# Transformer layer on one core: scores, states, own values and carried values of TensorE's batches put into one stretch of small tiles

## The reference, cut to what matters

```python
def _L0_attn_ref(hidden_states, rel_pos, Wq, Wk, Wv, Wo):     # 8 heads of 16
    q, k, v = (split_heads(hidden_states @ W) for W in (Wq, Wk, Wv))
    # per head, chunks of C = 64 tokens, gamma = 1 - 2**(-5-head):
    attn    = (qc @ kc.T) * D              # D = gamma**(i-j) where i >= j
    o_intra = attn @ vc
    o_inter = (qc * decay_q) @ S
    S_new   = decay_s * S + (kc * decay_k).T @ vc
    return o @ Wo

def _L0_ffn_ref(x, ...):
    h = bitlinear(x, w_fc) + gate * (x @ v.T @ fast_b.T @ u.T)
    r = maximum(h, 0)
    return bitlinear(r * r, w_proj)

xn = layernorm(x)                          # x: 8 x 512 x 128, float32
return x + attn(xn) + ffn(xn)
```

## Time and profile before

| what | value |
|---|---|
| median of 3 runs | 129.23 us (128.18 to 129.38) |
| the profiled execution's own time | 129.01 us |
| its span, from the first to the last instruction | 127.0 us |
| TensorE busy | 117.0 us (92%) |
| VectorE busy | 99.2 us (78%) |
| ScalarE busy | 78.7 us (62%) |
| GpSimd busy | 64.0 us (50%) |
| granted TensorE clock, mean | 0.997 |

### The profile page before, as it was taken

The page is one execution under the profiler, slowest core; times in us unless marked ns, Lnnn a source line. Parts: engine busy times, 40 slices in busy tenths (PEclk is TensorE's granted clock), DMA queues, the critical chain, the costliest instruction groups (busy, mean ns, idle before and its releaser), DMA issues.

```text
span 127.0 us, 6564 instructions
## 1 busy us (share of the span) xinstructions
PE 117.0 (92%) x2860; PEld 92.8 (73%) x2860; DVE 99.2 (78%) x261; ACT 78.7 (62%) x158; POOL 64.0 (50%) x60
## 2 busy tenths in 40 slices
PE   4979999988999999499999999999999999499991
PEld 4425869856688778377788778878897889377890
DVE  0788795489799969858699979896999799729832
ACT  3265669967871897227972897188738774382910
POOL 7099803984439161923439252916193529544400
PEclk9999999999999999999999999999999999999998
DMA  3849920000023000400023001300020002000202
GB/s 105 296 149 320 389 92 34 0 3 5 8 90 81 5 0 23 145 7 0 0 92 74 0 0 53 112 0 0 0 83 0 0 0 83 0 5 0 88 5 83
DMA packets 3357, 7.71 MB, mean 61 GB/s; under 512 B 384, under 2 KB 896, under 8 KB 3216
## 3 DMA queue, kind: packets, MB, share of 16 engines
q1 hardware_dynamic: 2880, 7.01, 16.3%
q10 hardware_dynamic: 464, 0.50, 1.2%
HBM read 5.42 MB, written 2.10 MB: 59 GB/s over the span
## 4 chain that ended last, share of the span: by engine, by line
PE 80%; DVE 10%; issue 4%; ACT 2%; POOL 1%; DVEq 0%; POOLq 0%
PE ps_work L659 10%; PE ps_score L735 8%; PE ps_work L663 7%; PE ps_work L660 7%; PE ps_score L705 6%; PE ps_score L747 5%; PE ps_score L781 5%; PE ps_y L761 4%; PE ps_y L762 4%; PE ps_score L720 3%; DVE sums_of L532 3%; PE ps_turn L668 3%; PE ps_y L765 2%; DVE xn L491 2%; PE ps_turn L692 1%
## 5 line engine op out<-in xcount | busy, mean ns | idle before, releaser
L300 POOL TENSOR_TENSOR sq_lo<-square,sq_hi 128x512 fp32r<-128x512 f32 x31 | 39.8, 1295 | 36.2 <-ACT sq_hi L356 36.2
L347 ACT ACTIVATE square<-ps_work 128x512 f32<-128x512 f32 x32 | 19.1, 596 | 23.1 <-PE ps_work L663 22.6
L516 DVE TENSOR_TENSOR scores<-ps_score,cst 128x512 f32<-128x512 f32 x32 | 20.3, 682 | 1.6 <-PE ps_score L705 1.6
L305 POOL TENSOR_TENSOR q_pair<-q_dec,cst 128x1024 f32<-128x1024 f32 x7 | 13.3, 1894 | 15.9 <-DVE q_dec L501 15.9
L356 ACT ACTIVATE sq_hi<-square 128x512 fp32r<-128x512 f32 x32 | 20.1, 627 | 0.1
L352 ACT ACTIVATE square<-square 128x512 f32<-128x512 f32 x32 | 18.9, 630 | 0.1
L491 DVE TENSOR_SCALAR xn<-x_in,mean_var,rstd 128x128 f32<-128x128 f32 x32 | 14.9, 528 | 0.3
L659 PE MATMUL ps_work<-xn_hi,w_hi 128*128 128x512 f32 x32 | 14.3, 447 | 0.4 <-issue 0.4
L735 PE MATMUL ps_score<-scores,v_pad 64*32 64x64 f32 x1024 | 12.5, 225 | 1.6 <-issue 1.6
L663 PE MATMUL ps_work<-xn_lo,w_hi 128*128 128x512 f32 x32 | 12.6, 394 | 0.0
L660 PE MATMUL ps_work<-xn_hi,w_lo 128*128 128x512 f32 x32 | 12.6, 393 | 0.0
(11 more groups left out here) (123 smaller groups left out, 238.6 us busy)
## 6 DMA issues: line engine op xcount, KB each, us to landing
x_in<-x_tok SPq DMA_DIRECT2D x8, 256.0 KB, 3.4
resid<-x_feat SPq DMA_DIRECT2D x1, 2048.0 KB, 7.7
out_feat<-resid SPq DMA_DIRECT2D x7, 256.0 KB
po_in<-ffn_weights SPq DMA_DIRECT2D x1, 320.0 KB, 3.2
fc_in<-ffn_weights SPq DMA_DIRECT2D x1, 256.0 KB, 3.7
q_table<-q_decay SPq DMA_DIRECT2D x1, 256.0 KB, 3.5
wqvk<-qvk_weights ACTq DMA_DIRECT2D x1, 192.0 KB, 3.9
cst<-const ACTq DMA_DIRECT2D x1, 129.0 KB, 3.9
```

What stands on the lines that cost most here:

```text
L300: nc.gpsimd.tensor_tensor(sq_lo[p][:, f, :], square[p][:, f, :], sq_hi[p][:, f, :].bitcast(F32), ALU.subtract).then_inc(lo_ready, 1)
L347: nc.scalar.activation(square[b.parity][:, f, :], ps_work[f % 2][:], ACT.Relu).then_inc(relu_ready, 1)
L516: nc.vector.tensor_tensor(scores[:, g].rearrange("p t s i -> p (t s) i"), ps_score[:, g].rearrange("p (a i) -> p a i", i=BLK), causal.unsq ...
```

## The change: what it does

- TensorE runs hidden 0 to 3 of b in a row. Then the four sets of small products stand in one stretch: score of b, gather states of b, own values of b - 1, carry of b - 1. Then turn of b + 1, second product and output product of b - 1, and q, k, v of b + 1.
- Own values go one batch later, so `scores` gets a second buffer. `own_values(first)` leaves the prologue; the code for the last batch holds own values twice (of batch 6 and of batch 7).
- PSUM: the attention output and the states move from ps_score into two banks of their own, ps_out. ps_turn and ps_y are now the third and fourth bank of ps_score, and the two v sides use its first and second. So turn, second product, q/k/v and score wait for the masks, for `take_v` and for `finish` that read those banks.
- VectorE's order in a body: statistics of b + 1, `take_v` of side 1 of b, variance, roots, normalise, four masks, `low_o`, `low_xn`, states of b and their sums, `decay_q`, `finish`, `take_v` of side 0. ScalarE takes all four relus before the squares. GpSimd's list is as it was.
- In the prologue VectorE copies w2, wo_full and wo_hi in place of ScalarE, and sums the states of batch 0 before it takes v of batch 1.

```diff
-        scores = sb("scores", [P, NG, NT, PAIR, BLK])
+        scores = [sb(f"scores{p}", [P, NG, NT, PAIR, BLK]) for p in range(2)]
...
         ps_score = pb("ps_score", [P, NG, SEQ])
+        ps_out = pb("ps_out", [P, ROWS, SEQ])
         ps_work = [pb(f"ps_work{p}", [P, SEQ]) for p in range(2)]
-        ps_turn = pb("ps_turn", [P, SEQ])
-        ps_y = pb("ps_y", [P, SEQ])
+        ps_turn, ps_y = ps_score[:, 2], ps_score[:, 3]
+
+        first_turn, ps_w1 = ps_out[:, 0], ps_out[:, 1]
...
-            return (ps_turn if side == 0 else other)[:].rearrange("p (w t d) -> p w t d", w=2, t=2)
+            if b is first:
+                bank = first_turn if side == 0 else ps_work[0][:]
+            else:
+                bank = ps_score[:, side]
+            return bank.rearrange("p (w t d) -> p w t d", w=2, t=2)
...
-        o_bank = ps_score[:, 0:ROWS, 0:NT * BLK].rearrange("p r (t i) -> p t r i", i=BLK)
+        o_bank = ps_out[:, :, 0:NT * BLK].rearrange("p r (t i) -> p t r i", i=BLK)
+        state_bank = ps_out[:, :, NT * BLK:NT * (BLK + GW)]
...
             take_relu(first, 3)
             round_xn(first.step(1))
             high_square(first, 0)
-            act.wait_ge(proj_turned, 1)
-            nc.scalar.activation(w2[:], ps_y[:].rearrange("p (t d) -> p t d", d=D), ACT.Copy).then_inc(w2_copied, 1)
             high_square(first, 1)
             take_square(first, 2)
-            act.wait_ge(wo_turned, 1)
-            nc.scalar.activation(wo_full[:], ps_y[:, 0:D], ACT.Copy)
-            nc.scalar.activation(wo_hi[:], ps_y[:, 0:D], ACT.Copy).then_inc(wo_rounded, 1)
-            take_square(first, 3)
-            high_square(first, 2)
             copy_k(first.step(1))
             copy_k_tok(first.step(1), 0)
+            take_square(first, 3)
             copy_k_tok(first.step(1), 1)
+            high_square(first, 2)
             high_square(first, 3)
 
             def body(b):
                 take_relu(b, 0)
                 take_relu(b, 1)
                 root(b.step(1))
-                take_square(b, 0)
-                take_square(b, 1)
-                high_square(b, 0)
+                take_relu(b, 2)
+                take_relu(b, 3)
+                for f in range(3):
+                    take_square(b, f)
+                    high_square(b, f)
                 high_o(b.step(-1))
-                take_relu(b, 2)
-                high_square(b, 1)
                 round_xn(b.step(1))
-                take_relu(b, 3)
-                take_square(b, 2)
                 take_square(b, 3)
-                high_square(b, 2)
+                high_square(b, 3)
                 copy_k(b.step(1))
                 copy_k_tok(b.step(1), 0)
-                high_square(b, 3)
                 copy_k_tok(b.step(1), 1)
...
-            take_relu(last, 0)
-            take_square(last, 0)
-            high_o(last.step(-1))
-            high_square(last, 0)
-            for f in range(1, NF):
+            for f in range(NF):
                 take_relu(last, f)
+            for f in range(3):
                 take_square(last, f)
                 high_square(last, f)
+            high_o(last.step(-1))
+            take_square(last, 3)
+            high_square(last, 3)
...
             nc.vector.tensor_scalar(wo_scaled[:], wo_in, inv_scale2[:], None, ALU.mult).then_inc(wo_ready, 1)
+            dve.wait_ge(proj_turned, 1)
+            nc.vector.tensor_copy(w2[:], ps_score[:, 1].rearrange("p (t d) -> p t d", d=D)).then_inc(w2_copied, 1)
             low_xn(after)
+            dve.wait_ge(wo_turned, 1)
+            nc.vector.tensor_copy(wo_full[:], ps_y[:, 0:D])
+            nc.vector.tensor_copy(wo_hi[:], ps_y[:, 0:D]).then_inc(wo_rounded, 1)
             decay_q(after)
             dve.wait_ge(wo_rounded, 1)
             nc.vector.tensor_tensor(wo_lo[:], ps_y[:, 0:D], wo_hi[:].bitcast(F32), ALU.subtract).then_inc(y_free, 1)
+            take_states(first)
+            for k in range(3):
+                add_states(first, k)
             take_v(after, 0)
-            take_v(after, 1)
             dve.wait_ge(resid_loaded, 16)
 
             def body(b):
                 before, after = b.step(-1), b.step(1)
                 statistics(after)
                 statistics_done(after)
-                take_states(before)
+                take_v(b, 1)
                 variance(after)
-                for k in range(3):
-                    add_states(before, k)
                 for step in range(4):
                     inverse_root(after, step)
                 normalise(after)
+                for g in MASK_ORDER:
+                    mask_scores(b, g)
                 low_o(before)
                 low_xn(after)
-                for g in MASK_ORDER[:2]:
-                    mask_scores(b, g)
+                take_states(b)
+                for k in range(3):
+                    add_states(b, k)
+                decay_q(after)
                 finish(before, ps_y)
-                decay_q(after)
-                for g in MASK_ORDER[2:]:
-                    mask_scores(b, g)
-                for side in range(2):
-                    take_v(after, side)
+                take_v(after, 0)
...
             before = last.step(-1)
-            take_states(before)
-            for k in range(3):
-                add_states(before, k)
-            low_o(before)
+            take_v(last, 1)
             for g in MASK_ORDER:
                 mask_scores(last, g)
-            finish(before, ps_y)
+            low_o(before)
             take_states(last)
             for k in range(3):
                 add_states(last, k)
@@ -645,6 +649,7 @@
             nc.vector.tensor_tensor(sq_lo[last.parity][:, NF - 1, :], square[last.parity][:, NF - 1, :],
                                     sq_hi[last.parity][:, NF - 1, :].bitcast(F32),
                                     ALU.subtract).then_inc(last_low_ready, 1)
+            finish(before, ps_y)
...
                 pe.wait_ge(xn_ready, b.count(1, 1))
+                if b is not first:
+
+                    pe.wait_ge(scores_ready, b.count(NG, 1 - NG))
...
+                if b is not first:
+                    pe.wait_ge(scores_ready, b.count(NG, 0))
+                elif side == 1:
                     pe.wait_ge(q_ready, b.count(1, 1))
-                elif side == 1:
-                    pe.wait_ge(y_free, b.count(1, 0))
...
                 pe.wait_ge(q_spread, b.count(PAIR, PAIR))
+                if b is not first:
+
+                    pe.wait_ge(v_ready, b.count(2, 2))
+                    pe.wait_ge(y_free, b.count(1, 0))
...
-
-                pe.wait_ge(scores_ready, b.count(NG, ROWS))
...
-                pe.wait_ge(scores_ready, b.count(NG, NG))
+                if b is last:
+                    pe.wait_ge(scores_ready, last.count(NG, NG))
+
+                    pe.wait_ge(state_step, last.count(3, 1))
...
-                pe.wait_ge(state_ready, b.count(1, 1))
+                if b is last:
+                    pe.wait_ge(state_ready, last.count(1, 1))
...
             pe.wait_ge(proj_ready, 1)
+            pe.wait_ge(scores_ready, NG)
...
             gather_states(first)
-            own_values(first)
             pe.wait_ge(wo_ready, 1)
-            pe.wait_ge(w2_copied, 1)
             nc.tensor.transpose(ps_y[:, 0:D], wo_scaled[:], ident).then_inc(wo_turned, 1)
...
-            def body(b):
-                before, after = b.step(-1), b.step(1)
+            def all_hidden(b):
 
                 pe.wait_ge(q_ready, b.count(1, 1))
                 hidden(b, 0)
                 pe.wait_ge(k_ready, b.count(1, 1))
-                hidden(b, 1)
-
-                pe.wait_ge(v_ready, b.count(2, 2))
+                for f in range(1, NF):
+                    hidden(b, f)
+
+            def small_tiles(b):
+                before = b.step(-1)
+
+                pe.wait_ge(scores_ready, before.count(NG, NG))
+                pe.wait_ge(state_ready, before.count(1, 1))
+                score(b)
+                gather_states(b)
+                own_values(before)
+                carry(before)
+
+            def body(b):
+                before, after = b.step(-1), b.step(1)
+                all_hidden(b)
+                small_tiles(b)
+                turn_xn(after)
+
+                pe.wait_ge(scores_ready, b.count(NG, 2))
                 second_product(before, ps_y, range(NF))
-                carry(before)
-                hidden(b, 2)
-                hidden(b, 3)
-                turn_xn(after)
                 pe.wait_ge(o_lo_ready, before.count(1, 1))
-                score(b)
                 output_product(before, ps_y)
                 project_q(after, b)
                 project_k(after, b)
                 project_vk(after, 0)
                 project_vk(after, 1)
-                gather_states(b)
-                own_values(b)
 
             over_batches(pe, body)
 
 
             before = last.step(-1)
-            pe.wait_ge(q_ready, last.count(1, 1))
```

(21 more changed lines are left out.)

54 lines of the change are left out of this document (28 added, 26 removed).

## The result

The changed kernel takes 139.2 us (median of four runs, 138.87 to 141.51), the kernel before 128.7 beside it: 1.081 times as long, 95% interval 1.071 to 1.092. The run of 141.51 was in a slower state, and the ratio leaves it out. The forecast was 126.5. The profiled execution took 139.48 us with a span of 137.4.

The account below looks back on a forecast made before the run. TensorE's own work was taken to bound the steady bodies, with waits at both ends; savings of 0.6 + 0.65 + 0.05 + 0.4 + 1.05 = 2.75 took 129.01 to 126.26, forecast as a 126.5 us median, range 124.3 to 128.9.

Parts of the forecast that it names:

- Steady bodies: Batches 3 to 6: 13.10 us less 0.41 for borders plus 0.27 for hidden 2 gives 12.97; minus 0.6 in all.
- Rival D: Steady bodies win nothing, with inner borders at 0.2 and hidden 2 waiting in every body: 128.2 us, chance 0.10.
- Prologue: Up to batch 1: own values leave (minus 1.40), later transposes, xn_lo wait and restarts add 0.28, 0.2, 0.2; minus 0.65.
- The end: Everything behind the last batch's last product, from 123.30 to the span's end, was to stay as it was.
- Batch 1: First body: two new waits, hidden 2 for a relu and score for v; 14.97 for 15.02 us, minus 0.05.
- I leave the pause with what surrounds it, 1.9: Batch 2: body of 12.97 plus 1.9 for the unchanged pause and its surroundings gives 14.88 us, minus 0.4.
- Last batch: 15.42 us to its last product: sums wait goes, own values of batch 6 come in (plus 1.40); minus 1.05 in all.
- one stretch less and smaller gaps: minus 0.5: Last batch: one stretch of small tiles less and smaller gaps were to save 0.5 us.
- The wait of 1.61 for the sums: Last batch: TensorE's 1.61 us wait for the states' sums was to go, as they are done a batch earlier.
- Rival A: Batch 2's pause, if tied to a number of instructions, disappears: minus 1.65 more, 124.8 us, chance 0.22.
- B: The longer stretch of small products brings one pause more, in batch 1: plus 1.7, 128.2 us, chance 0.16.
- Rival C: VectorE, waiting for GpSimd operations, becomes the bound in the bodies: six of 13.8, 131 us, slower than before, chance 0.09.

Follow-up runs that it names:

- The second profile of the changed kernel: The changed kernel with 128 no-operations at the front of TensorE's list, which left its instruction counts as they were: 139.11 us.

## Why the prediction was wrong

The steps in its own order.

**Steady bodies: right.** 12.93 and 12.88 us, 12.97 was said. Three stretches into one saves the two outer borders, hidden 2 gives 0.27 back, inner borders cost nothing. Rival D falls with that. So does the rule of the Trainium skill, "TensorEngine Tiling (Array Packing)", Tiling Modes, as a price: it says that each change of mode drains the array, and score to gather (32x64 to 64x32) is such a change; here no extra time shows at it (1.14 us for the 64 products of score, up to gather as up to a wide one).

**Prologue: right**, 8.38 for 8.36 (its terms as written add up to 0.72 and not to 0.65, which it called rounding for the slots). **The end: right**, 3.75 for 3.70.

**Batch 1: right but for the pause.** 14.97 was said, 17.26 came, and 2.36 of it is the pause; without it 14.90. Both data waits are there at their sizes: hidden 2 idle for 0.73, score for 1.03, the three sums at 3.8 us where 3.6 was said.

**Batch 2: the step "I leave the pause with what surrounds it, 1.9".** It came as two, 0.86 and 1.76 idle, for 1.64.

**Last batch: wrong, and here is most of the loss.** 14.37 was said, 22.09 came. 5.46 us are three pauses of which the sum had none, 1.4 the half clock behind the last of them, and about 0.9 the order itself, whose "one stretch less and smaller gaps: minus 0.5" I cannot find in the trace. The wait of 1.61 for the sums did go.

**The start: not in the sum.** 2.46 us later than in the profile of before. The second profile of the changed kernel had 0.6. It is scatter: hidden 0 of batch 0 lay between 15.9 and 18.5 in the kernels that leave that part as it was, one of 19.81 apart.

**What failed is the treatment of the earlier trace rows.** I saw a pause, took it rightly for instructions that had not come, and then counted it as one fixed piece of 1.64 that could stay, go (A), or double (B, once, in batch 1, 128.2 us). B had the right mechanism, small products that run instructions through fastest, though it read it off a pause that was not of that kind: the block before it lasted 4.4 us, and its packet was late. That was in part luck. And B had a price for one pause, a chance of 0.16, and nothing on the last batch, which is all new code with the same stretch in it and own values twice. Six pauses came, 10.44 us where the sum had the one of 1.64. What would have given the count was in the trace of before: eleven packets for some 2980 instructions of code, one each time a block is entered, 2.3 us from asking to the start behind a pause, against 608 instructions in 4 us. By that, two or three pauses in every first run of the stretch could be expected, and the loop's later turns free, as they were.

Rival A is refuted in its form. The Trainium skill, in "Runtime: NRT & Kernel Launch", Instruction fetch mechanics, gives TensorE room for 2048 instructions, refilled in blocks of 256; I had taken the first figure for the place of the pause. The trace agrees with the second: pauses a multiple of 256 apart, to one instruction, in every kernel here with more than one. The page also says that the cost of crossing a block's end is mostly hidden. That holds where wide products run, and fails in small ones, by 0.4 to 2.4 us each time. Rival C did not come: VectorE is busy 11.45 of 12.93 us in batch 3, and TensorE never waits for it there.

## What to carry to other kernels

Count TensorE's instructions as well as its microseconds. In code that runs for the first time, some 256 instructions (a small product and its weight load are two) that took well under 3.5 us ended in a pause of up to 2.4 us in these kernels, so wide products between small sets do a job that no timeline of a loop's later turns shows; gathering small products into one stretch saved 0.2 us a stretch in the steady loop and lost 8.8 us of pauses outside it. Before unrolling a loop or writing out a last iteration of its own, add that price.
